# A state-space layer whose gate projection moves in front of the loop over pairs of heads

## What is computed

```python
proj = x @ Win.T
x_ssm = proj[..., :H * P].reshape(B, T, H, P)
z = proj[..., H * P:2 * H * P].reshape(B, T, H, P)
Bm, Cm = ...
dt = jax.nn.softplus(dt_raw + dt_bias)
xc = jax.nn.silu(_causal_conv(x_ssm, conv_w_x))
Bc = jax.nn.silu(_causal_conv(Bm, conv_w_b))
Cc = jax.nn.silu(_causal_conv(Cm, conv_w_c))
decay = jnp.exp(dt * A)
...
y = y * jax.lax.rsqrt(jnp.mean(y * y, axis=-1, keepdims=True) + 1e-06)
y = y * jax.nn.silu(z)
return y.reshape(B, T, H * P) @ Wout.T
```

## Time and profile before

| | before |
|---|---|
| median of 3 runs | 2190.05 us (2181.96 to 2190.75) |
| the profiled execution: its own time | 2183.36 us |
| the profiled execution: span of the core | 2181.3 us |
| PE busy | 1675.2 us, 77% of the span |
| DVE busy | 1427.0 us, 65% |
| ACT busy | 736.8 us, 34% |
| POOL busy | 482.9 us, 22% |
| state-space layer, first block | from 26.1 to 50.9 us of the span |
| state-space layer, loop over pairs | from 51.0 to 560.6 us of the span |

### The profile page before, as it was taken

One profiled execution on the slowest core, in us unless ns is written; L12 is line 12 of the kernel. 1 busy time (PEld: TensorE's weight loads), 2 busy tenths in 40 slices (PEclk: granted clock), 3 DMA queues, 4 the chain that ended last, 5 costly groups with the idle time before them and its releaser, 6 DMA issues. The chain is left out here.

```text
span 2181.3 us, 33781 instructions
## 1 busy us (share of the span) xinstructions
PE 1675.2 (77%) x12017; PEld 1263.0 (58%) x12046; DVE 1427.0 (65%) x2363; ACT 736.8 (34%) x1162; POOL 482.9 (22%) x572
## 2 busy tenths in 40 slices
PE   2899999998886976366666478899995988888353
PEld 2688888887763663122455234688884875556221
DVE  3677877787325855899575754434445993677977
ACT  0466555665221531233133112333331002335111
POOL 0233333332001401476031003200000322143000
PEclk9999999999997986588878678899996997989555
DMA  2000000000000000000100020000001210100000
GB/s 107 23 30 14 29 29 29 29 29 8 0 0 21 2 7 32 0 0 0 41 4 12 15 96 4 9 0 0 0 0 58 72 43 27 50 3 2 1 0 19
DMA packets 13049, 46.09 MB, mean 21 GB/s; under 512 B 1699, under 2 KB 2340, under 8 KB 11686
## 3 DMA queue, kind: packets, MB, share of 16 engines
q1 hardware_dynamic: 12966, 44.96, 6.1%
HBM read 43.91 MB, written 1.05 MB: 21 GB/s over the span
## 5 line engine op out<-in xcount | busy, mean ns | idle before, releaser
L2008 DVE SCALAR_TENSOR_TENSOR arena<-psum,arena 128x1016 f32<-128x1016 f32 (+2 forms) x240 | 303.9, 1267 | 99.8 <-ACT arena L1944 94.1
L858 DVE TENSOR_REDUCE limits<-psum 128x4 f32<-128x512 f32 (+2 forms) x256 | 148.3, 620 | 92.8 <-PE psum L718 57.3
L1839 PE MATMUL psum<-ssm_XT_hi,ssm_split 128*128 128x512 f32 x640 | 196.3, 409 | 16.0 <-POOL ssm_split L1797 11.1
L826 ACT ACTIVATE PT<-psum 128x1024 f32<-128x1024 f32 x112 | 108.6, 1021 | 120.4 <-PE psum L749 120.4
L718 PE MATMUL psum<-K,QR 32*128 32x256 f32 (+1 forms) x320 | 123.9, 470 | 26.8 <-POOL K L694 16.8
L1944 ACT ACTIVATE arena<-psum,arena 128x1024 f32<-128x1024 f32 x80 | 89.0, 1112 | 158.2 <-PE psum L1839 158.2
L1839 PEld LDWEIGHTS psum<-ssm_XT_hi,ssm_split 128*128 128x128 f32 x640 | 117.4, 193 | 38.4 <-POOL ssm_split L1797 14.5
L2354 PE MATMUL psum<-expert,x 128*128 128x256 f16 x1024 | 114.4, 276 | 16.8 <-POOL expert L2340 16.8
L1796 POOL TENSOR_TENSOR ssm_split<-arena,const 128x256 fp32r<-128x256 f32 x80 | 58.4, 730 | 291.0 <-DMA arena<-in_ssm_in 166.6
L2492 POOL TENSOR_TENSOR fed<-dtx,b_all 128x1024 f32<-128x1024 f32 x32 | 103.1, 3243 | 77.5 <-ACT b_all L2541 44.1
L2354 PEld LDWEIGHTS psum<-expert,x 128*128 128x128 f16 x1024 | 101.4, 99 | 29.7 <-issue 16.9
(11 more groups left out here) (413 smaller groups left out, 3725.7 us busy)
## 6 DMA issues: line engine op xcount, KB each, us to landing
arena<-in_ssm_in SPq DMA_DIRECT2D x32, 384.0 KB, 3.3
expert_mask<-in_expert_masks SPq DMA_DIRECT2D x32, 256.0 KB, 2.6
arena<-in_L_xattn SPq DMA_DIRECT2D x1, 5120.0 KB, 16.1
arena<-in_L_ffn SPq DMA_DIRECT2D x1, 2592.0 KB, 10.2
arena<-in_L_xattn SPq DMA_DIRECT2D x2, 1280.0 KB, 6.3
arena<-in_L_attn SPq DMA_DIRECT2D x1, 2272.0 KB
arena<-in_L_ffn SPq DMA_DIRECT2D x1, 2176.0 KB, 8.8
arena<-in_L_xattn SPq DMA_DIRECT2D x1, 1667.0 KB, 6.9
```

The lines of the kernel that those rows point to most:

```text
L826: nc.scalar.activation(PT[:, u % 2, 2 * k:2 * k + 2, :, :].rearrange("p r h q -> p (r h q)"), p.psum[:, (2 + 2 * k) * 512:(4 + 2 * k) * 51 ...
L858: ins = nc.vector.tensor_reduce(limits[:, u % 2, r, :, k], score_bank(r)[:, :].rearrange("p (h k) -> p h k", h=4)[:, :, lo:hi], AX.X, ALU. ...
L1839: ins = nc.tensor.matmul(bank[tile_bank(r, tile) + half][:, :], w_part(tile, kw, c), x_part(kx, c, slice(half * 512, (half + 1) * 512)), s ...
L2008: ins = nc.vector.scalar_tensor_tensor(out[:, :, ago:], product[:, :, :P - ago], tap, out[:, :, ago:], ALU.mult, ALU.add)
```

## The change

The weights of the gate leave the tensor that the loop loads and get a tensor of their own, `ssm_z`, in four groups of four pairs. Four DMAs of 512 KB load them in the first block, into the part of `gated` that is written last. POOL splits each group into a rounded part and a rest. PE makes 32 tiles of 128 tokens x 512 gate columns, 6 matmuls of 512 columns each, 16 tiles ahead of the sums over time and 16 behind, in banks 4 to 7 in turn; ACT applies silu to each. ACT instead of DVE makes `XT_hi`, and DVE makes `XT_lo` at the block's start. In the loop `project_z`, its silu and its waits are gone. Products use banks 5, 6, 7 and 6, only group 3 waits for a mix (that of group 1), and products and outputs stand in twos. ACT's and DVE's lists are written in another order too, and the second half of a pair's weights is loaded as soon as POOL has split the pair before.

```diff
             with ExitStack() as first, nc.Block(no_gpsimd_drain=True) as block:
+                z_split = [[first.enter_context(nc.sbuf_tensor(f"ssm_z{r}{k}", [P, T], F32R)) for k in range(2)] for r in range(2)]
...
                 def _(sync):
+                    for g in range(4):
+                        sync.dma_start(z_raw[g].rearrange("p (c n) -> p c n", c=DC), p.dram["ssm_z"][g]).then_inc(s.loaded.up(16), 16)
                     p.load_next(sync)
+
+                @block.gpsimd
+                def _(pool):
+                    ones8 = p.c("ones").rearrange("p (o n) -> p o n", o=1).broadcast_to([P, 8, P])
+                    for g in range(4):
+                        if g == 0:
+                            pool.wait_ge(s.loaded.sem, s.loaded.at(63))
+                        if g >= 2:
+                            pool.wait_ge(s.z_psum.sem, s.z_psum.at(8 * (g - 2) + 7))
+                        hi, lo = (a[:, :] for a in z_split[g % 2])
+                        p.pool_chain.then(pool, nc.gpsimd.tensor_tensor(hi.rearrange("p (o n) -> p o n", n=P), z_raw[g].rearrange("p (o n) -> p o n", n=P), ones8, ALU.mult))
+                        nc.gpsimd.tensor_tensor(lo, z_raw[g], hi.bitcast(F32), ALU.subtract).then_inc(s.split_ready.up(), 1)
...
+                    def project_z(g, b):
+                        n = 8 * g + b
...
+                        if n >= 4:
+                            pe.wait_ge(s.z_ready.sem, s.z_ready.at(n - 4))
+                        products = [(kw, kx, c) for kw, kx in ((0, 0), (0, 1), (1, 0)) for c in range(DC)]
+                        for kw, kx, c in products:
+                            ins = nc.tensor.matmul(z_bank(n)[:, :], (XT_hi, XT_lo)[kx][:, c, b * P:(b + 1) * P],
+                                                   z_split[g % 2][kw][:, :].rearrange("p (c n) -> p c n", c=DC)[:, c, :],
+                                                   start=(kw, kx, c) == products[0], stop=(kw, kx, c) == products[-1])
+                        ins.then_inc(s.z_psum.up(), 1)
...
                     ins.then_inc(s.tile_ready.up(), 1)
+                    for n in range(16):
+                        project_z(n // 8, n % 8)
                     pe.wait_ge(s.dt_ready.sem, s.dt_ready.at(0))
...
+                    for n in range(16, 32):
+                        project_z(n // 8, n % 8)
...
                 def _(act):
+                    nc.scalar.copy(XT_hi[:, :, :], p.XT[:, :, :]).then_inc(s.x_ready.up(), 1)
...
+                    for n in range(32):
+                        g, b = divmod(n, 8)
+                        act.wait_ge(s.z_psum.sem, s.z_psum.at(n))
+                        nc.scalar.activation(gated[:, 4 * g:4 * g + 4, b * P:(b + 1) * P], z_bank(n)[:, :].rearrange("p (k n) -> p k n", k=4), ACT.Silu
+                                             ).then_inc(s.z_ready.up(), 1)
...
-                product_bank = lambda g: bank[5] if g < 2 else bank[6]
+                product_bank = lambda g: bank[(5, 6, 7, 6)[g]]
...
-                            pe.wait_ge(s.mixed_ready.sem, s.mixed_ready.at(n + -1))
+                            if g == 3:
+                                pe.wait_ge(s.mixed_ready.sem, s.mixed_ready.at(n + -2))
```

```diff
                         if has_b:
                             mix(2)
-                        if has_a:
-                            weigh_x(0)
-                            convolve(m, r, 3)
-                        if has_b:
                             mix(3)
                         if has_a:
+                            convolve(m, r, 3)
+                            weigh_x(0)
+                            convolve(m, r, 4)
                             weigh_x(1)
-                            convolve(m, r, 4)
```

More of the change, by code:

```diff
@@ L1667, in state_space @@
             dtx = spare(2, B, P)
-            bc = [[spare(T) if (r, k) == (1, 3) else sb2(f"bc{r}{k}", [P, T])[:, :] for k in range(TILES - 1)] for r in range(2)]
+            early = [sb2(f"bc0{k}", [P, T])[:, :] for k in range(2)]
+            late = spare(T)
             XT_hi = sb2("XT_hi", [P, DC, T], F32R)
@@ L1685, in state_space @@
             assert taken[0] <= ARENA[1]
-            with nc.Block(no_gpsimd_drain=True) as block:
+            with ExitStack() as first, nc.Block(no_gpsimd_drain=True) as block:
+                z_split = [[first.enter_context(nc.sbuf_tensor(f"ssm_z{r}{k}", [P, T], F32R)) for k in range(2)] for r in range(2)]
                 row = lambda t: t.rearrange("p (o n) -> p o n", o=1).broadcast_to([P, B, SSM_H])
+                z_raw = [gated[:, 12 + g, :] for g in range(4)]
+                z_bank = lambda n: bank[4 + n % 4]
@@ L1741, in state_space @@
             p.close()
+            bc = [early + [sb2(f"bc0{k}", [P, T])[:, :] for k in (2, 3)], [sb2(f"bc1{k}", [P, T])[:, :] for k in range(3)] + [late]]
             def steps(engine, emit, chain=None, links=0):
@@ L1855, in decay_sums @@
                             ins.then_inc(s.decay_psum.up(trips), 1)
[L1857 to L1862, removed]
-                            ins.then_inc(s.z_psum.up(trips), 1)
                         def products(g):
                             n = m * 4 + (g - 4)
-                            pe.wait_ge(s.mixed_ready.sem, s.mixed_ready.at(n + -1))
+                            if g == 3:
+                                pe.wait_ge(s.mixed_ready.sem, s.mixed_ready.at(n + -2))
                             for q in range(4):
@@ L1913, in step @@
                         if has_b:
+                            outputs(0)
                             outputs(1)
-                            pe.wait_ge(s.z_ready.sem, s.z_ready.at(m + -1))
                             products(2)
+                            products(3)
+                        if has_a:
+                            project(m, r, 3)
+                        if has_b:
+                            outputs(2)
+                            outputs(3)
                         if has_a:
@@ L1988, in step @@
                             nc.scalar.activation(square[:, :], p.psum[:, 4 * 512:6 * 512], ACT.Square).then_inc(s.square_ready.up(trips), 1)
+                        if has_a:
+                            silu(m, r, 3)
+                            tap(m, r, 4)
                         if has_next:
```

53 lines of the change are left out of this document (20 added, 33 removed).

## The result

The changed kernel takes 2215.27 us (2214.58 to 2216.47, 4 runs) against 2188.58 us (2181.96 to 2190.75, 4 runs) before: a ratio of 1.0128, 95% interval 1.0105 to 1.0151, so slower by 1.3%. The direction was forecast, the size was not: +15.6 us and a range to 2215 were predicted, +26.7 us were measured.

What follows compares the result with a forecast made beforehand. PE bounded the loop before; afterwards DVE's chain with ACT would, at 28.65 us a pair. First block +39.8 and loop -24.2 make +15.6 us, on a mean of 2186.5 giving 2202 us, range 2189 to 2215.

Steps and rivals of the forecast that it cites:

- What PE loses: In each pair of the loop, PE loses the gate's projection, 3.57 us; its busy time falls from 28.35 to 24.8 us.
- PE is the bound: Loop of the kernel before: PE, busy 28.52 of 30 us with short waits, sets the 29.82 us a pair.
- DVE's chain, 28.65 us: New loop period: DVE's tiles plus three gaps for ACT's taps, 1.17 less than 29.82; 14 periods give 16.4 less.
- PE's own path, 8.85 against 9.05 us: From second weighing through decay sums, project, products to second mix: 8.85; DVE's path to tile 1 is longer by 0.2.
- a wait of 3 us at the decay sums: Sign that the forecast is right: PE idle 3 us at the decay sums in the loop, ended by `weigh_x`.
- My rows for slow matmuls: Lower-clock allowances: 1.8 us after PE's idle time in the first block, 1.1 us for pair 15's first products.
- Rival 3: In the loop, PE's path outlasts DVE's: +0.3 to +0.65 us a pair, 4 to 9 us, 2206 to 2211; chance 0.22.
- The first block, +39.8: Ahead of the loop: gate weights' DMAs, splits, 192 matmuls and sums over time start the loop 39.8 us later.
- Pair 0 and pair 15: Loop's ends: pair 0 loses 1.0 us through its table load, pair 15's lone half 6.8 us.
- The base: Whole kernel before: mean of four times, 2186.5 us, to which the forecast change of +15.6 was added.
- The table load and the step of a matmul: Table load's whole switch lies in the 3.45 us first gap, without 1.38 drain; gate matmuls step by 236, not 215.7 ns.
- Slower by over 0.5%: Whole kernel: more than 11 us slower, covering the forecast and two rivals; chance 0.74.

Runs made afterwards that it cites:

- Experiment 5: Kernel before with only the gate's tiles moved in front of the loop, old lists of PE, ACT and DVE and old banks kept: 2221.02 us, 1.0138.
- experiment 6: Changed kernel plus 10 matmuls without a use in PE's wait for the second weighing: 2201.51 us, 1.0048 to before.
- Experiment 1: Changed kernel with DVE weighing the second half of x ahead of tile 4's convolution instead of behind it: 2194.24 us, 1.0014 to before.
- experiment 2: Changed kernel with ACT's taps of tiles 3 and 4 ahead of the silus of tiles 2 and 3: 2186.94 us, 0.9977 to before.
- the first experiments: The first four follow-up sets, in which the unchanged kernel before was also timed: 2191.54 us over 18 runs.
- experiment 3: Changed kernel with both the second weighing ahead of tile 4 and taps of tiles 3 and 4 ahead of silus: 2176.71 us, 0.9929 to before.

## Why the prediction was right and wrong

**What PE loses, and why the loop doesn't get it.** Right. 3.57 us less work on PE bring almost nothing while the three engines wait for each other. Experiment 5 has it alone, 0.3 us a pair, and 0.5 at the full clock. The prediction's words for the kernel before, that PE is the bound, say too much: DVE's waits of 2.0, 2.1 and 0.9 us for ACT stood in its period as well.

**DVE's chain, 28.65 us.** Right as a sum: the five short periods are 28.6 to 28.7, and with the clock held all 14 are (experiment 6). The gaps stood in pair 0 of the kernel before, and they returned: the wait ahead of tile 3 is the 2.13 less 1.2 for two mixes, 0.93. Experiment 1 takes the weighing out of the sum, experiment 2 half of the two later waits.

**PE's own path, 8.85 against 9.05 us.** This is the step that failed. The sum was right for a PE at its full clock, and I wrote down a wait of 3 us at the decay sums as a sign that the forecast was right. But I priced only the wait and not the matmuls behind it. They came at 1.2 GHz in nine periods of 14 and took 1.65 us more, some eight times the slack. The kernel before had rows for such a price: after a wait of 2.60 us in its first pair PE's matmuls grew slow (timeline of PE, kernel before):

```profile
66.21 0.70 PE L1839 MATMUL psum<-ssm_XT_hi,ssm_split 128*128 128x512 f32 x2 [2.60 <-DVE arena L2008]
66.75 0.89 PE L1839 MATMUL psum<-ssm_XT_lo,ssm_split 128*128 128x512 f32 x2
67.44 1.91 PE L1839 MATMUL psum<-ssm_XT_hi,ssm_split 128*128 128x512 f32 x4
```

Four such matmuls take 1.08 us at the full clock. My rows for slow matmuls went into the first block and pair 15 only. In numbers: 9 x 1.34 = 12.1 of the 12.5 us between -3.9 and -16.4. Rival 3, that PE's path wins the tie, was the true one, but it had 0.22 and its price of 0.3 to 0.65 a pair, taken from one short wait, was too low: the mean is 0.88.

**The first block, +39.8.** +37.7. POOL started at 34.67 (34.6 forecast), PE at 39.48 (39.4), with slow matmuls for its first 4 us. The tiles took 1.40 and not 1.46 us each: the wait at a tile's head, which a project has, was not there.

**Pair 0 and pair 15.** -3.3 instead of -1.0, and -6.5 instead of -6.8. In pair 0 PE's matmuls grew slow in four stretches before and in two after, the first one of the loop in both; I had kept the slow ones whole. In pair 15 the total is right, but its parts are not shown: in experiment 5, where the gate's matmuls are gone and the old lists stand, the stretch takes 24.07 us at a granted clock of 0.57, against 22.07 at 0.90 before, so the 4.1 us for the gate did not come by themselves.

**The base.** I took the mean of four times, 2186.5. The 18 runs of the first experiments put the median of before at 2191.5. These 5 us are the rest of the distance from 2202 to 2215: 12.5 for the periods, less 2.1 for the block and 2.3 for pair 0, 0.3 for pair 15 and 5.0 for the base make 13.4. So the time lay just over the range's upper end, 2215, by two misses that add up, the clock and the base.

**The table load and the step of a matmul.** The table load's place in the sum was right: with 1.38 us more in the gap no period could have been 28.7, so no run shows the drain that the Trainium skill (ScalarE: Activation LUTs, "What ACT_TABLE_LOAD costs") puts behind it. The gate's tiles took 1.40 us for six matmuls, 233 ns each, and the rows of the kernel before had given 236. The Trainium skill (TensorE: Matmul & The Clock Gate, "Wait — 56ns, not 53.3ns?") has 215.7 ns from one matmul of 512 columns to the next; the trace doesn't reach that here.

**Faster, same, slower.** Slower by over 0.5% had 0.74, and came, for the reason that was given: the block cost more than the loop won, 37.7 us against 13.7.

## What to carry to other kernels

Work taken from the busiest engine comes back only if the engines that it feeds don't wait for each other in a ring: follow one engine through a period in the new order, and put each thing that another engine waits for ahead of what nobody waits for. Here taps ahead of silus, with what that did to the clock, took 28 us off the changed kernel, while the move with the old lists had added 30 us to the kernel before. Where a sum leaves an idle time on TensorE, price the matmuls behind it at both clock levels before calling a path the shorter one; a slack below that difference is none. And take the time of before from many runs, not from the profiled one.

## What the runs showed of the hardware

**More matmuls, less time.** A wait of 2.8 us on PE was followed by matmuls at half the clock in two pairs of three, at the same place in the program, and ten matmuls without a use in that wait made the kernel 13.8 us faster. After the waits of 2.0 us in experiment 2 it still happened, in three pairs of 14. In experiments 1 and 3 the decay sums wait for nothing, and yet four and two periods of 28.6 are left, all with a granted clock of 0.94. In the first of the two of experiment 3 the slow matmuls stand behind the outputs, which had waited 1.1 us for the mix (timeline of PE; four matmuls of a tile take 1.20 and 1.05 us there where two lines of 0.71 and 0.63 are the rule):

```profile
333.07 2.09 PE L1922 MATMUL psum<-arena,X 128*128 128x64 f32 x16 [1.10 <-DVE X L2050]
...
335.67 1.20 PE L1887 MATMUL psum<-ssm_XT_hi,ssm_split 128*128 128x512 f32 x2
336.67 1.05 PE L1887 MATMUL psum<-ssm_XT_lo,ssm_split 128*128 128x512 f32 x2
```

The same wait, 0.91 to 1.13 us, stands there in all 14 pairs of that run, and twelve show no such effect, so the length of a wait alone doesn't tell where the clock falls. What a period at 0.94 costs depends on whose path it hits: 0.5 us in experiments 1 and 5, 1.3 in the changed kernel and in experiment 2, 1.6 in experiment 3, the quickest of the five.

**POOL holds DVE up.** In the changed kernel's first block DVE's small instructions lasted as long as POOL's long ones beside them (timelines of POOL and of DVE):

```profile
34.67 2.34 POOL L1711 TENSOR_TENSOR ssm_z<-ssm_gated,const 128x1024 fp32r<-128x1024 f32 x1 [34.22 <-DMA ssm_gated<-in_ssm_z]
37.09 2.34 POOL L1712 TENSOR_TENSOR ssm_z<-ssm_gated,ssm_z 128x1024 fp32r<-128x1024 f32 x1
```

```profile
34.69 2.47 DVE L2647 TENSOR_SCALAR arena<-arena 128x256 f32<-128x256 f32 x1 [0.48 <-ACT arena L1751]
37.19 2.52 DVE L2649 SCALAR_TENSOR_TENSOR arena<-arena 128x256 f32<-128x256 f32 x1
```

The second kind takes 0.42 us alone (its shortest of nine), and the nine took 10.32 us instead of 4.10. The Trainium skill (SBUF — State Buffer, "Who interferes with whom") says that DVE and POOL share a pair of ports that one of them holds for a whole instruction, and that a DVE instruction with two inputs in SBUF needs it. The trace agrees: `SCALAR_TENSOR_TENSOR` on two SBUF inputs ends 0.3 us behind POOL's instruction beside it. `TENSOR_SCALAR`, with one such input, was held as well, 2.47 us instead of 0.29 before. It cost nothing here, since PE came to the sums over time at 63.6 only, but the softplus was ready at 49.5 instead of 41. DVE's convolutions, which read PSUM and SBUF, took 3.87 us for three beside POOL as without it.
